# Transposing the quantised row tiles by DMA instead of TensorE in a fused cross-attention and FFN block

## What is computed

```
x = x + tanh(g_xattn) * xattn(layernorm(x), ctx)
xq = clip(round(layernorm(x) / sx), -128, 127) * sx          # sx from the maximum over all x
gate, up = xq @ Wq_gate.T, xq @ Wq_up.T                      # rows x 1408 each
h = silu(gate) * up
hq = clip(round(h / sh), -128, 127) * sh                     # sh from the maximum over all h
x = x + tanh(g_ffn) * (hq @ Wq_down.T)
```

## Time and profile before

| | |
|---|---|
| median of 3 runs | 1384.22 us |
| lowest and highest run | 1378.6 and 1385.66 us |
| the profiled execution's own time | 1385.78 us |
| its span, from the first to the last instruction | 1384.0 us |
| mean granted TensorE clock over the span | 0.957 of full speed |
| gate and up, the loop over row blocks | about 1145 to 1298 us in the span |

### The profile page before, as it was taken

The page is one execution under the profiler, slowest core; times in us unless marked ns, Lnnn a source line. Parts: engine busy times, 40 slices in busy tenths (PEclk is TensorE's granted clock), DMA queues, the critical chain, the costliest instruction groups (busy, mean ns, idle before and its releaser), DMA issues.

```text
span 1384.0 us, 17169 instructions
## 1 busy us (share of the span) xinstructions
PE 1131.9 (82%) x7075; PEld 362.5 (26%) x7075; DVE 1165.5 (84%) x1668; ACT 1257.5 (91%) x484; POOL 14.0 (1%) x32
## 2 busy tenths in 40 slices
PE   6887688788666887689798798796676679999998
PEld 5321112112111221122122122121111145444443
DVE  7688899986999899788989888777899948888777
ACT  5799999999999999999999999999999956656595
POOL 4000000000000000000000000000000000000000
PEclk9899889999898999899999999999989889999999
DMA  6000011100110001000000100000000013411196
GB/s 222 1 16 1 31 51 56 53 10 16 39 38 24 23 16 36 0 1 0 0 22 21 45 0 1 1 0 0 1 1 0 1 31 130 153 53 47 58 342 231
DMA packets 29875, 61.47 MB, mean 44 GB/s; under 512 B 3771, under 2 KB 5835, under 8 KB 29797
## 3 DMA queue, kind: packets, MB, share of 16 engines
q1 hardware_dynamic: 28896, 60.04, 13.2%
q10 hardware_dynamic: 197, 0.32, 0.1%
q0 software_dynamic: 704, 0.01, 0.0%
HBM read 46.20 MB, written 14.16 MB: 44 GB/s over the span
## 4 chain that ended last, share of the span: by engine, by line
ACT 72%; PE 20%; DVE 8%; issue 1%; DMA 0%; SPq 0%; DVEq 0%
ACT big L519 71%; PE ps L1225 11%; PE ps L1245 5%; DVE big L722 4%; PE ps L1034 1%; PE ps L1191 1%; DVE bn L647 1%; PE ps L1096 1%; PE ps L1205 1%; PE ps L1091 0%; DVE wgu L655 0%; DMA wgu<-in_x_dram 0%; PE ps L1023 0%; PE ps L1047 0%; DVE block_sums L765 0%
## 5 line engine op out<-in xcount | busy, mean ns | idle before, releaser
L519 ACT ACTIVATE big<-big 128x6144 f32<-128x6144 f32 x204 | 1056.8, 5268 | 7.5 <-DVE big L722 7.5
L722 DVE TENSOR_SCALAR big<-big,atxt 128x1536 f32<-128x1536 f32 (+2 forms) x915 | 794.4, 921 | 121.0 <-PE ps L1091 116.9
L1091 PE MATMUL ps<-big,wslide 128*32 128x512 f32 x4312 | 614.3, 628 | 187.8 <-ACT big L519 180.9
L1091 PEld LDWEIGHTS ps<-big,wslide 128*32 128x32 f32 x4312 | 132.5, 112 | 607.7 <-ACT big L519 313.0
L1225 PE MATMUL ps<-aux,wgu 128*128 128x512 bf16 x680 | 151.5, 379 | 0.0
L1034 PE MATMUL ps<-big,aux 128*128 128x512 f32 x256 | 144.4, 652 | 2.5 <-ACT big L461 1.6
L1096 PE MATMUL ps<-big,wslide 128*32 128x512 f32 x616 | 89.5, 697 | 43.2 <-ACT big L519 43.1
L566 ACT ACTIVATE aux<-ps,sgux 128x512 f32<-128x512 f32 x88 | 60.0, 686 | 56.7 <-PE ps L1225 55.8
L978 DVE SCALAR_TENSOR_TENSOR big<-ps,sgux,aux 128x512 f32<-128x512 f32 x88 | 65.9, 749 | 26.4 <-PE ps L1225 17.3
L1225 PEld LDWEIGHTS ps<-aux,wgu 128*128 128x128 bf16 x680 | 65.3, 98 | 73.4
L1245 PE MATMUL ps<-wd,wgu 128*128 128x512 bf16 x352 | 76.1, 379 | 0.0
(11 more groups left out here) (164 smaller groups left out, 443.3 us busy)
## 6 DMA issues: line engine op xcount, KB each, us to landing
aux<-in_x_dram SPq DMA_DIRECT2D x96, 256.0 KB, 2.7
out_dram<-aux SPq DMA_DIRECT2D x32, 256.0 KB, 3.5
hidden_spill<-big SPq DMA_DIRECT2D x6, 768.0 KB, 5.5
big<-hidden_spill SPq DMA_DIRECT2D x6, 768.0 KB, 7.2
wgu<-in_x_dram SPq DMA_DIRECT2D x11, 256.0 KB, 7.3
aux<-in_L_ffn_w_gate_dram SPq DMA_DIRECT2D x11, 256.0 KB, 2.7
aux<-in_L_ffn_w_up_dram SPq DMA_DIRECT2D x11, 256.0 KB, 3.0
aux<-in_L_ffn_w_down_dram SPq DMA_DIRECT2D x4, 704.0 KB, 4.1
```

The costliest lines, as they stand in the source:

```text
L519: nc.scalar.activation(unit, unit, ACT.Tanh).then_inc(tanh_done, 1)
L722: v.tensor_scalar(ring[:, place(p)], src, atxt[:, e, bt * T + t:bt * T + t + 1], None, ALU.add).then_inc(sums_ready, 1)
L1091: last = mm(bank(k)[32 * part:32 * part + 32, :], wslide[:, e, 31 - g:63 - g], unit[:, part * 512:(part + 1) * 512], start=(e == 0 and g = ...
```

## The change

The tiles of block 0 are transposed on TensorE as before. For tiles 4 to 31 (blocks 1 to 7) SP issues one DMA transpose a tile, from `xq` in SBUF to `xqT` in SBUF, and TensorE's four transposes and ScalarE's copy of the tile are gone. PE waits for the DMAs' semaphore `xqT_in` (16 for each) at the start of a block, DVE waits for it before it writes over an `xq` buffer, and SP waits, before a transpose, until the tile is quantised and until all transposes before it have landed. In SP's stream the transpose of tile n - 3 stands right behind the load of tile n; the last three stand behind all loads. The four store cuts of a spilled block are issued with the loads of tiles 4(r+3) to 4(r+3)+3 instead of 4(r+2) to 4(r+2)+3, and stand behind the transpose of that turn.

```diff
+            def transpose_in(n):
+                rb, j = n // 4, n % 4
+                sp.wait_ge(xq_ready, n + 1)
+                if n > 4:
+                    sp.wait_ge(xqT_in, 16 * (n - 4))
+                if rb >= 2 and j == 0:
+                    sp.wait_ge(up_done, IC * (rb - 1))
+                sp.dma_start_transpose(xqT[:, rb % 2, :, j * P:(j + 1) * P], xq[:, n % 2, :]).then_inc(xqT_in, 16)
+
             for n in range(TILES):
                 if n >= 3:
                     sp.wait_ge(xu_ready, n - 2)
                 sp.dma_start(xt[:, n % 3, :], x_rows[n * P:(n + 1) * P, :]).then_inc(xt_in[n % 3], 16)
-                r, c = n // 4 - 2, n % 4
+                if n - 3 >= 4:
+                    transpose_in(n - 3)
+                r, c = n // 4 - 3, n % 4
                 if 0 <= r < SPILLED:
                     sp.wait_ge(h_ready, IC * (r + 1))
                     cut = slice(*cuts[c])
                     sp.dma_start(h_spill[r][:, cut, :], h_slots[:, r, cut, :]).then_inc(h_stored[r], 16)
 
+
+            for n in range(TILES - 3, TILES):
+                transpose_in(n)
...
             def copy_xqT(n):
                 rb, j = n // 4, n % 4
                 act.wait_ge(xq_transposed, n + 1)
-                if rb >= 2 and j == 0:
-                    act.wait_ge(up_done, IC * (rb - 1))
...
-                    if rb + 1 < RB and i in (3, 5, 7, 9):
-                        copy_xqT(4 * (rb + 1) + i // 2 - 1)
...
             def quantise_x(n):
                 dve.wait_ge(xu_ready, n + 1)
-                if n >= 2:
+                if 2 <= n < 6:
                     dve.wait_ge(xq_transposed, n - 1)
+                if n >= 6:
+                    dve.wait_ge(xqT_in, 16 * (n - 5))
...
             for rb in range(RB):
-                pe.wait_ge(xqT_ready, 4 * (rb + 1))
+                if rb:
+                    pe.wait_ge(xqT_in, 64 * rb)
+                else:
+                    pe.wait_ge(xqT_ready, 4)
...
-                    turns = (4, 5, 7, 9) if rb == 0 else (2, 4, 6, 8)
-                    if rb + 1 < RB and i in turns:
-                        transpose_xq(4 * (rb + 1) + turns.index(i))
```

More of the change, by code:

```diff
@@ L217, in flamingo_gated_block @@
         xqT_ready = sem("xqT_ready")
+        xqT_in = sem("xqT_in")
         gate_done = sem("gate_done")
```

## The result

| | before | after |
|---|---|---|
| median | 1384.42 us (16 runs) | 1377.6 us (16 runs) |
| lowest and highest | 1378.6 and 1386.51 | 1372.32 and 1380.32 |
| profiled execution, own time and span | 1385.78, 1384.0 | 1375.13, 1373.2 |
| loop over row blocks, first matmul to the next group | 153.0 us | 146.9 us |

The ratio is 0.9955, 95% interval 0.9943 to 0.9967: 0.45% less. The prediction was 1378 us and 0.46%.

A forecast was written before the change was run, and what follows sets the result against it. TensorE was taken to bound the gate and up stage; dropping its transposes saves 7 x 0.92 = 6.4 us, other terms nothing, so 1384.2 - 6.4 = 1378 us against the median. The range was 1374 to 1415 us.

The forecast's parts named there:

- TensorE is the bound and its transposes are the gain: Gate and up stage: TensorE sets the pace; removing its transposes from seven blocks, 0.92 us each, gains 6.4 us.
- ScalarE's copies and the moved stores are worth nothing: Gate and up stage: 28 copies (16.5 us) are hidden behind TensorE; moving the stores gains nothing by itself.
- The stores had to move: SP's queue: at their old place SP waits for block 0's end, tiles 6 and 7's transposes behind it; block 1 starts late.
- L = 2.7 us, from the load of a tile: SP's serial transposes: time from one's issue to the next's, between 2.4 and 6.0 us, taken from a 256 KB load's median.
- The small pieces that I feared: DMA transposes write small pieces, which can cost more than bytes: a 0.2 KB mask load in tiny pieces takes 6.0 us.
- The figure of 1309 ns for a 128x128 square: DMA transposes: if a tile's four squares went one after another, a turn would be 5.24 us, the time some 1420 us.
- The bounds 3.07 and 3.82 us: Longest time per transpose, issue to next issue, with nothing late for TensorE: 3.07 us in block 0, 3.82 us in others.
- "about 5 us": Block 3: time the last clip leaves the fourth tile's transpose before TensorE wants it.
- Stores among the transposes at no cost: Blocks 1 to 3, SP's queue: stores between transposes of tiles 9 to 16 taken as nothing; upper bound 13 us.
- 28L - 104: Starts of blocks 1 to 7: TensorE's total stall in us, L being the time from one transpose's issue to the next's.
- the slower rival: Block starts: the serial chain of transposes is the new bound; +16 us at 4.5 us a transpose, +36 at 5.24; chance 0.34.
- the clock, priced at up to 3.4 us a block: TensorE after idling over 2 us at a block's start: lower granted clock, up to 7 x 3.4 = 24 us on top.

The follow-up runs named there:

- the doubled kernel: Changed kernel with each DMA transpose of a tile done twice, the second when the first has landed: 1439.08 us, ratio 1.0395.
- the doubled kernel with dummies: Changed kernel with each DMA transpose done twice, plus 60 dummy matmuls on TensorE ahead of its wait at blocks 1 to 7: 1434.83 us, ratio 1.0385.

## Why the prediction was right, step by step

- **TensorE is the bound and its transposes are the gain.** Right, and shown from both sides: put back beside the DMAs they cost 153.0 - 146.9 = 6.1 us, left out of the kernel before they give 153.0 - 146.8 = 6.25. Predicted 6.4, measured 6.1. The price came from differences of group starts (0.2155 us a wide matmul, 0.23 us for four transposes), not from the 10.8 us of busy time. A block became 0.90 us shorter (19.89 to 18.99), not 0.92.
- **ScalarE's copies and the moved stores are worth nothing.** Right: the kernel without transposes keeps the copies and loses nothing by them, and moving the stores alone gave a ratio of 1.0003.
- **The stores had to move.** Right in kind; TensorE waits 20.4 us at the old place, where my sum ahead of the run had 15.
- **L = 2.7 us, from the load of a tile.** Measured 2.5, and landing 2.4. The value was near, the reason for it less so, and in that there is some luck. I argued from bytes (half of a load's), and the runs show that size doesn't enter between one square and four. The small pieces that I feared (the page counts 19004 packets under 512 B, before 3771) cost nothing that can be seen.
- **The figure of 1309 ns for a 128x128 square** (the Trainium skill, VectorE: DVE Perf Modes, section The three transpose paths). Four squares in series would have given an estimated 5.24 us, and this case doesn't bear it out for squares of one DMA: a tile of four lands in 2.4 us. It is near SP's 1.2 us for one instruction, but no run here shows what was measured there. The rule of the Trainium skill (Advanced Engine Details and Errata, section X-Bar Transpose (TRN2)) that such DMAs are as fast as ordinary ones agrees with the landing (2.4 us for 128 KB, against 2.7 for a load of 256 KB) and not with the issue (1.2 us of SP against 0.33 to 0.58).
- **The bounds 3.07 and 3.82 us.** As bounds on a chain that is longer than the clips' spacing they hold: with L = 3.67 block 1 waits 3.04 us (2.4 by the formula), with 5.0 it waits 7.50 (7.7 by the formula), and with 6.2 the seven waits add up to 68.2 us (70). But at the L that was met the chain doesn't set the time. The last clip does, which the prediction looked at for the other blocks ("about 5 us") and not for block 0. There the room was 0.9 us, and two slow transposes used it up, which cost the 0.14 us. That the gain came whole at this place was a near thing.
- **Stores among the transposes at no cost.** Right while the chain is not the bound. Once it is, four of the eight stores add some 1.6 us each to a turn and a fifth 0.8 (the doubled kernel).
- **28L - 104 for the slower rival, plus the clock.** It gave +36 us at L = 5.0, and the doubled kernel lost 61. The sizes that failed are the slow transposes, taken as nothing (11 us, most of it behind stores), and the clock, priced at up to 3.4 us a block: it acted on the end with 12 us in seven blocks, through the first clips and the last block's matmuls. The formula itself was met where neither disturbs, 23.79 us against 23.7.
- **A slip in the sum of that rival.** At L = 4.5 it has 1394 to 1420 us. By its own terms it is 1384.2 + 15.6 = 1400 us, and 1424 with the 24 us for the clock. The forecast doesn't hang on it.

## What to carry over

When work is moved off a saturated engine, the gain is its share of that engine's stream, read from differences of group starts. Whether it is kept is decided by two bounds that the old trace already holds: how long after the first input is ready the consumer wants the last one, divided by the transfers in series between; and how long after the last input is ready it wants it, for one transfer. The first decides when transfers are slower than their inputs come, the second when they are faster, as here. Work out both first, for the tightest place; then an unknown duration need only be placed on one side of them. A DMA transpose is paid by the instruction, so give it as many squares as can wait (four was the most tried), and look at what else stands in the same queue: a wait for each of two blocks, harmless among loads, cost 20 us once a critical DMA stood behind it.

## What the runs showed of the hardware

- A DMA transpose from SBUF to SBUF occupied SP for 1.2 us and landed 2.4 us from its issue whether it moved one 128x128 bf16 square or four; two in series were 2.5 us apart.
- Right behind a 768 KB store and a tile's load, the same transpose took 4.1 us to the next issue; behind the 512 KB store of a block's last cut it took 2.7 and 3.3. Without a store near, five of 19 in the changed kernel took 3.1 to 4.0 us, each with a packet on an "instruction" queue in its time.
- In the doubled kernel with dummies, TensorE's matmuls of a block took 18.9 us behind idle times listed as 1.5 to 2.3 us and 20.6 to 21.6 us behind idle times listed as 2.5 to 6.0 us. The length of the gap alone doesn't decide: ahead of the stage TensorE idles 2.6 us, and behind that the granted clock stood at 0.50 in the kernel before and at 1.00 in the kernels with the stores moved and with the transposes kept. In the doubled kernel it stood at 0.50 (1.2 GHz) in the first microseconds of a block behind a long wait:

```profile
1160.37:1164.00 3.63, 3.63 (x9) 1.33 (x10) 0.00 (x0) 0.69 (x1) 0.00 (x0) 0.50 0.21 76
1164.00:1168.00 4.00, 4.00 (x18) 1.69 (x17) 3.08 (x5) 2.08 (x3) 0.00 (x0) 0.89 0.16 33
```
